# The front of an attention and feed-forward kernel: biases through TensorE, weights one transfer at a time, filling with 512-column products, and a normalisation moved behind a softmax step

## What is computed

```python
def _proj(W, b, x):
    return jnp.einsum('oi,bil->bol', W, x) + b[:, None]
q, k, v = _proj(Wq, bq, ln(x)), _proj(Wk, bk, ctx), _proj(Wv, bv, ctx)     # heads: 8 blocks of 64 columns
scores = jnp.einsum('hbdk,hbek->hbde', qh, kh) / 8
x = x + _proj(Wo, bo, softmax(scores) @ vh)
h = ln(x)
x = x + (silu(h @ deq(gate)) * (h @ deq(up))) @ deq(down)                  # 512 -> 1792 -> 512
deq(w) = (w - zeros of its group) * scales of its group                    # groups of 128 rows
```

## Time and profile before

| | |
|---|---|
| three runs | 451.0, 453.35, 453.71 us; median 453.35 us |
| the profiled execution | 453.45 us, of which the span from first to last instruction is 451.6 us |
| mean granted TensorE clock | 0.981 |
| busy share of the span | PE 93%, ACT 74%, DVE 72%, POOL 60% |
| DMA | 35.52 MB, mean 79 GB/s |
| the front | the first 56 us, up to PE's first L743 |

### The profile page before, as it was taken

One profiled execution on the slowest core, in us unless ns is written; L12 is line 12 of the kernel. 1 busy time (PEld: TensorE's weight loads), 2 busy tenths in 40 slices (PEclk: granted clock), 3 DMA queues, 4 the chain that ended last, 5 costly groups with the idle time before them and its releaser, 6 DMA issues.

```text
span 451.6 us, 10920 instructions
## 1 busy us (share of the span) xinstructions
PE 418.6 (93%) x4318; PEld 328.4 (73%) x4318; DVE 327.0 (72%) x576; ACT 332.9 (74%) x542; POOL 271.4 (60%) x269
## 2 busy tenths in 40 slices
PE   4979898999797799999999899999999999999994
PEld 4857765777584587877777677877778888888873
DVE  2765742999688776878877766877877666666676
ACT  2215699779676788777877858787879999888970
POOL 4145397779858664657555654655656556555561
PEclk8869999999999999999999989999999999999999
DMA  7984343876464100000201000000010000000003
GB/s 196 360 281 137 100 135 129 287 228 228 142 232 137 29 2 25 1 25 1 73 25 48 0 1 25 4 24 3 23 44 6 1 2 0 23 25 23 25 1 93
DMA packets 26918, 35.52 MB, mean 79 GB/s; under 512 B 1963, under 2 KB 18515, under 8 KB 26867
## 3 DMA queue, kind: packets, MB, share of 16 engines
q1 hardware_dynamic: 26354, 34.69, 23.4%
q0 software_dynamic: 192, 0.07, 0.4%
q10 hardware_dynamic: 320, 0.07, 0.1%
HBM read 30.63 MB, written 4.19 MB: 77 GB/s over the span
## 4 chain that ended last, share of the span: by engine, by line
PE 68%; POOL 10%; issue 8%; DVE 5%; ACT 5%; DMA 3%; POOLq 0%; SPq 0%; DVEq 0%; ACTq 0%
PE banks L743 19%; PE banks L745 17%; PE banks L756 9%; PE banks L757 9%; PE banks L641 3%; POOL t_sb L406 3%; PE banks L774 2%; DVE yT L978 2%; POOL hr L419 2%; DMA x_sb<-in_x 2%; PE banks L659 2%; PE banks L681 2%; PE banks L670 2%; PE banks L651 2%; ACT banks L543 1%
## 5 line engine op out<-in xcount | busy, mean ns | idle before, releaser
L543 ACT ACTIVATE banks<-banks,ratio 128x512 f32<-128x512 f32 x336 | 208.3, 665 | 36.9 <-PE banks L745 25.9
L978 DVE SCALAR_TENSOR_TENSOR yT<-banks,sd,yT 128x512 f32<-128x512 f32 x208 | 154.4, 747 | 45.8 <-PE banks L757 45.5
L743 PE MATMUL banks<-xT,wgu 128*128 128x512 f32 x448 | 182.9, 408 | 3.9 <-DVE t_sb L963 2.7
L745 PE MATMUL banks<-xT,wgu 128*128 128x512 f32 x448 | 175.7, 392 | 0.0
L406 POOL TENSOR_TENSOR t_sb<-t_sb,u_sb 128x512 f32<-128x512 f32 x56 | 72.9, 1302 | 92.8 <-DVE t_sb L963 92.5
L743 PEld LDWEIGHTS banks<-xT,wgu 128*128 128x128 f32 x448 | 84.5, 189 | 25.7 <-ACT banks L543 3.3
L756 PE MATMUL banks<-hr,wd 128*128 128x512 f32 x224 | 89.8, 401 | 9.5 <-DVE yT L978 6.1
L745 PEld LDWEIGHTS banks<-xT,wgu 128*128 128x128 f32 x448 | 84.7, 189 | 15.4
L757 PE MATMUL banks<-hr,wd 128*128 128x512 f32 x224 | 87.8, 392 | 0.0
L419 POOL TENSOR_TENSOR hr<-t_sb,hr 128x512 fp32r<-128x512 f32 x56 | 72.2, 1289 | 5.1 <-ACT hr L565 0.7
L756 PEld LDWEIGHTS banks<-hr,wd 128*128 128x128 f32 x224 | 42.2, 188 | 25.7 <-DVE yT L978 13.7
(11 more groups left out here) (88 smaller groups left out, 402.1 us busy)
## 6 DMA issues: line engine op xcount, KB each, us to landing
x_sb<-in_x SPq DMA_DIRECT2D x16, 256.0 KB, 5.4
out<-x_sb SPq DMA_DIRECT2D x16, 256.0 KB, 2.2
wgu_in<-in_L_ffn_gate_w SPq DMA_DIRECT2D x7, 512.0 KB, 6.6
z_in<-in_L_ffn_gate_z SPq DMA_DIRECT2D x7, 512.0 KB, 4.9
wgu_in<-in_L_ffn_up_w SPq DMA_DIRECT2D x7, 512.0 KB, 7.1
z_in<-in_L_ffn_up_z SPq DMA_DIRECT2D x7, 512.0 KB, 5.2
wd_in<-in_L_ffn_down_w SPq DMA_DIRECT2D x7, 512.0 KB, 5.5
z_in<-in_L_ffn_down_z SPq DMA_DIRECT2D x7, 512.0 KB, 4.3
```

The lines of the kernel that those rows point to most:

```text
L543: act.activation(banks[:, bank, :], banks[:, bank, :], ACT.Copy, scale=ratio[:, m, g, it:it + 1]).then_inc(done[n % 2], 1)
L743: pe.matmul(banks[:, bank, :], w, xT[:, c % 2, 0, g, :], start=g == 0, stop=False, skip_group_check=True)
L745: pe.matmul(banks[:, bank, :], w, xT[:, c % 2, 1, g, :], start=False, stop=True, skip_group_check=True).then_inc(full[n % 2], 1)
L978: dve.scalar_tensor_tensor(y, bank, sd[:, it, b:b + 1], y, ALU.mult, ALU.add).then_inc(s_free, 1)
```

## The change

1. **Biases.** POOL's six bias transfers become two. `bv` and `bo` come as one row each from POOL, `bq` and `bk` as one row each from ACT's queue, between the weights `Wq`, `Wk` and `Wv`, `Wo`. PE spreads them: a product of a row of ones with the two rows gives `bq` and `bk` on 128 partitions (L792 of the new file), four products with one column give `bv` and `bo`. DVE copies both results to where they stood before.
2. **Loads.** SP issues context tile 1 and x tile 2 ahead of the scales. For the first four pieces it waits until the integers have landed before it issues the zeros, and until these have landed before it issues the next piece. x tiles 3 to 5 and context tiles 3 to 5 stand in the same list.
3. **Filling.** One `stir` step is now a full float32 product of 512 columns instead of a transpose of 128. The counts go from 16 to 4, from 12 to 3, from 22 to 5, from 7, 6 and 5 to 1.
4. **ACT.** `norm2(j-2)` runs in step j behind the exponential and `norm1`, where it stood at the end of step j-1.
5. **DVE.** `take_w(0)`, which copies the turned `Wq` and `Wk`, runs before `stats(0, 1)`, not behind it.

```diff
@@ sync
-            load_x(0)
-            load_ctx(0)
-            load_x(1)
+            for t in range(2):
+                load_x(t)
+                load_ctx(t)
+            load_x(2)
             sync.dma_start(s_raw[0:NG * NI, 0, :], gate_s.rearrange("g (t p) -> (g t) p", p=P)).then_inc(s_sc, 16)
...
-            load_ctx(1)
-            load_x(2)
-            load_w(0)
-            load_zeros(0)
             load_ctx(2)
             load_x(3)
-            load_w(1)
-            load_zeros(1)
-            load_ctx(3)
-            load_x(PRE)
-            load_ctx(PRE)
-            for k in range(2, NP):
+
+            for k in range(EARLY):
                 load_w(k)
-                if k == 3:
-                    load_x(PRE + 1)
-                    load_ctx(PRE + 1)
+                if 1 <= k < 3:
+                    (load_ctx if k == 1 else load_x)(k + 2)
+                sync.wait_ge(s_w[k], 16)
+                load_zeros(k)
+                if k == 2:
+                    load_ctx(PRE)
+                wait_zeros(sync, k)
+            load_x(PRE + 1)
+            load_ctx(PRE + 1)
+            for k in range(EARLY, NP):
+                load_w(k)
@@ gpsimd
-            for m, v in enumerate((bq, bk)):
-                pool.dma_start(bqk[:, m, :],
-                               v.rearrange("(a o) -> a o", a=1).partition_broadcast(P)).then_inc(s_bias, 16)
-            for h in range(2):
-                for m, v in enumerate((bv, bo)):
-                    pool.dma_start(bvo[h * D:(h + 1) * D, m:m + 1],
-                                   v.rearrange("(o a) -> o a", a=1)).then_inc(s_bvo, 16)
+            pool.memset(ones, 1.0).then_inc(s_id, 1)
+            for m, v in enumerate((bv, bo)):
+                pool.dma_start(b_row[:, 2 + m, :], v.rearrange("(a o) -> a o", a=1)).then_inc(s_bvo, 16)
@@ scalar
             load(s_wsm, wraw[:, 1, :], Wk)
+            for m, v in enumerate((bq, bk)):
+                load(s_bias, b_row[:, m, :], v.rearrange("(a o) -> a o", a=1))
             load(s_wsm2, wraw[:, 2, :], Wv)
...
                 if j + 2 <= PRE:
                     norm1(j + 2)
+                if j >= 2:
+                    norm2(j - 2)
...
                     convert(j - 1)
-                if j >= 1:
+                if j == PRE - 1:
                     norm2(j - 1)
@@ tensor
                 for _ in range(n):
-                    pe.transpose(banks[:, bank, 3 * P:4 * P], ident[:, :], ident[:, :])
+                    pe.matmul(blocks(bank), ident[:, :], ident[:, :].unsqueeze(1).to_broadcast([P, NC, P]),
+                              start=True, stop=True)
             pe.wait_ge(s_id, 2)
-            stir(16)
+            stir(4)
...
-            stir(6)
+            pe.wait_ge(s_id, 4)
+            pe.wait_ge(s_bias, 32)
+            pe.matmul(banks[:, 7, 0:2 * D], ones, b_row[:, 0:2, :], start=True, stop=True).then_inc(s_brow, 1)
+            stir(1)
             pe.wait_ge(s_wT, 1)
             project(0)
-            stir(12)
+            stir(3)
             score(0)
...
+            pe.wait_ge(s_bvo, 32)
+            for m in range(2):
+                for r in HALVES:
+                    mm = pe.matmul(banks[r, 7, 4 * D + m:4 * D + m + 1], b_row[:, 2 + m, :], ones[:, 0:1],
+                                   start=True, stop=True)
             mm.then_inc(s_tr, 1)
...
             turn_x(PRE - 2)
-            stir(22)
+            stir(5)
...
-            stir(7, U_BANK[1])
+            stir(1, U_BANK[1])
@@ vector
+            take_w(0)
             stats(0, 1)
-            take_w(0)
             shift(0, 1)
-            dve.wait_ge(s_bias, 32)
+            dve.wait_ge(s_brow, 1)
+            dve.tensor_copy(bqk[:, :, :].rearrange("p m o -> p (m o)"), banks[:, 7, 0:2 * D]).then_inc(s_bqk, 1)
+            dve.wait_ge(s_bqk, 1)
             take_qk(0, 0)
...
                     take_w(1)
+                    dve.tensor_copy(bvo[:, :], banks[:, 7, 4 * D:4 * D + 2]).then_inc(s_wT, 1)
+                    dve.wait_ge(s_wT, 3)
```

## The result

| | before | changed |
|---|---|---|
| median of the comparison | 452.56 us (4 runs) | 447.20 us (4 runs, 446.94 to 447.67) |
| ratio | | 0.9884, interval 0.9856 to 0.9913 |
| profiled execution, span | 453.45, 451.6 us | 446.94, 445.1 us |
| first feed-forward product | 55.97 us | 50.00 us |

A forecast was written before the change was run, and what follows sets the result against it. PE was taken as nearly the only bound of the front; stage times put its first feed-forward product at 50.1 instead of 55.97 us, carried unchanged to the end: 453.45 - 5.85 = 447.6 us, range 444.5 to 452.5.

The forecast's parts named there:

- Opening: PE's start up to `mix(0)`: projection at 9.0 instead of 10.79, `mix(0)` at 20.0 instead of 21.87, a gain of 1.9 us.
- C: Rival, opening: wide products raise the clock no sooner, it runs at half speed as before; 452.6 us, chance 0.10.
- Price of a filling product: PE's filling: 0.87 us per 512-column product, 1.7 at half clock; five products instead of 22 transposes cost 1.8 us.
- loss of 1.0: At `score(3)`: x tile 4 lands late, q and k are ready at 31.2 where PE could start at 30.2.
- Stall and clock: `mix(0)` to `mix(1)`: the 3.26 us idle and the half clock go, 7.2 us instead of 13.0, `mix(1)` at 27.2.
- Behind weight transfers: The 3.26 us idle in `mix(0)`: PE waits for its own program, held up by weight transfers on the DMA engines.
- B: Rival, `mix(0)`: the stall stays, a matter of PE's list and not of DMA load; 453.2 us, chance 0.12.
- This needs the stall gone: Condition for `mix(1)` 7.7 us earlier: only one 512 KB transfer and a tile in flight from 12 to 40 us.
- Loads one at a time: SP's chain of loads: 4.1 us a step, first integers landing at 10, x tile 4 at 27.4, 1.0 us lost.
- D: Rival, slower: chain of loads too long, PE idles 5 us for x tile 4, clock falls; 454.1 us, chance 0.10.
- E: Rival, main loop takes part back: zeros 4 to 6 come late by 2 to 3 us; 450 us, chance 0.08.
- ACT: Second normalisation moved from in front of tile 2's exponential: exponentials of tiles 2 and 3 come 0.7 us earlier.

The follow-up runs named there:

- after_again: The changed kernel once more, unedited, on another chip: 446.90 us, ratio to before 0.9897.
- x4_early: The changed kernel with x tile 4 issued right behind the first integers and context tile 4 behind the second: 448.89 us, ratio to before 0.9926.
- u_fill: The changed kernel with transposes of 128 columns for filling again, in the old counts: 447.63 us, ratio to before 0.9884.
- x4_lean: As x4_narrow, also without the filling in front of `score(j + 1)` and `values(j)`: 442.69 us, ratio to before 0.9793.
- o_loads: The kernel before with only SP's new list of loads: 449.63 us, ratio to before 0.9946.
- u_bias: The changed kernel with the six bias transfers on POOL's queue again and no bias products on PE: 452.76 us, ratio to before 1.0003.
- x4_bare: As x4_lean, with all filling behind the first 16 transposes dropped: 445.57 us, ratio to before 0.9850.
- u_loads: The changed kernel with SP's old list, the weight transfers issued at once again: 451.78 us, ratio to before 0.9992.
- o_bias: The kernel before with only the biases as rows spread by PE and the two copies on DVE: 449.09 us, ratio to before 0.9941.
- tail3: The changed kernel with three filling products instead of five ahead of the last tile's turning: 445.96 us, ratio to before 0.9858.
- u_norm: The changed kernel with ACT's second normalisation at the end of the step before again: 450.42 us, ratio to before 0.9934.
- x4_narrow: As x4_early, with filling by transposes in the old counts: 443.68 us, ratio to before 0.9800.

## Why the prediction was right, step by step

**The whole.** Forecast 447.6 us, measured 447.2; the first feed-forward product forecast for 50.1, measured at 50.00; faster at 1.2%, to which I gave 0.55. The comparison's own median of before was 452.56, so against it the gain is 5.4 us, and against the profiled execution 453.45 - 446.94 = 6.5 us, where the sum had 5.85.

**Opening.** Four products ended at 7.77 (forecast 7.5), the projection began at 9.62 (9.0), `mix(0)` at 20.13 (20.0). That the engine starts at half speed and rises under the products is what the rows show, and the projection ran at full speed. When it rises is partly luck: the same four products ended at 6.7 us in after_again and at 6.6 in x4_early. What the forecast missed is that narrow filling lets the projection start sooner still, at 7.43 in u_fill. C did not come; it spoke of the half speed "as before", but before the clock had been up at 6.82 and fell again at 8.0.

**Price of a filling product.** Five in a row took 48.65 - 44.36 = 4.29 us, 0.86 each, as forecast (0.87). A single one between other stages takes 1.05, from its start to the next row's. That term was undersized by 0.18 us in each of some 14 places, and nearly all of them are on PE's path. It shows in the first step: `mix(0)` to `mix(1)` took 8.01 us, forecast 7.2, with four fillings at 1.05 and 0.32 us of waiting for DVE, so `mix(1)` came at 28.14 and not at 27.2. It does not show at the end, because the later steps were taken too long: `mix(1)` to `mix(2)` 8.02 (8.65, with a loss of 1.0 that did not come), `mix(2)` to `mix(3)` 5.40 (5.65), the rest 8.44 (8.6). With 0.13 us more in the opening the errors are +0.94 and -1.04 us. That 50.1 met 50.00 so closely is luck.

**Stall and clock.** Right in what it is, and the central point, but only partly right in what sets it. The idle without a semaphore came in the kernel before and in eleven of the twelve experiment kernels after 222, 347 or 348, or 474 records of PE: 126 or 127 records apart, whatever stage stood there; the one after 726 in x4_lean is three such steps behind 348. With its weight load a record is two instructions, so 127 records are some 254. The Trainium skill (Runtime: NRT & Kernel Launch, "Instruction fetch mechanics") has blocks of 16 KiB with 256 instructions and calls the crossing "mostly hidden"; the spacing and the packet's 0.02 MB agree, the hiding does not: 0.2 to 3.3 us were seen here. The instruction queue settles it. In each of these 22 idles (0.17 us and more) PE goes on 1.2 to 1.6 us after the end of a 16 KB packet of that queue (end of the packet and start of PE: 24.39 and 25.70 us in the kernel before, 22.72 and 24.16 in o_loads, 25.29 and 26.85 in after_again), and in the changed kernel's first profile, which has no such idle, the packet had ended 1.7 us before record 347 was due. So PE waits for its program. Two short idles of 0.38 and 0.54 us (after 402 records in u_bias, 796 in x4_bare) have no such packet and are not explained.

"Behind weight transfers" is the part that holds less well. With the weight transfers at once (before, u_loads, o_bias) the packets of the boundaries at 347 or 348 and 474 began 4.0 to 4.2 us after PE had crossed the boundary before, in one case 2.3; with loads one at a time mostly 0.7 to 3.2 us, in one case 4.7. The idles of a front add up to 3.3 to 5.7 us in the first group and to 0 to 2.6 in the second. So crowding goes with longer idles, but they come without it: 2.26 us in o_loads at a DMA share of 0.11, and 1.7 to 2.0 us after 474 records in after_again, tail3, x4_early and u_norm. B, a matter of PE's list, was right to that extent. The step "This needs the stall gone" held for the profiled execution, not for every one.

**Loads one at a time.** x tile 4 was forecast at 27.4; DVE started on it at 27.45. The steps of the chain were 3.7 to 4.1 us. The first integers landed at 11.1 and not at 10, which the shorter steps and a tile that took 4.0 us instead of 4.7 made good. The loss of 1.0 us I had put at `score(3)` did not appear: q and k were ready at 31.2 as forecast, but the longer filling brought PE to `score(3)` at 31.50 only.

**D**, the chain too long, was given 0.10 and did not occur in the profile, but its mechanism did in three others: in u_bias, u_fill and o_loads PE idled 4.0 to 4.3 us for x tile 4, and the clock fell, as the rival had it. In u_norm, tail3 and after_again DVE waited 2.0 to 2.5 us and PE did not idle for it. Against the changed kernel u_bias lost 5.6 us where 6.5 had been worked out. **B** and **E** did not come in the changed kernel; x4_narrow, with a front 5.4 us shorter, did give some back in the main loop, through waits for POOL. **ACT** was right at 0.6 us by the waits (u_norm), with the rest of that run's median open.

## What to carry to other kernels

Price a transfer that is issued behind waits by everything queued behind it: six bias transfers of 0.07 MB cost 5.6 us in the changed kernel, where each piece waits for the last (u_bias), and 0.6%, some 3 us, in the kernel before, which has no such chain (o_bias). Filling on PE is worth its place only up to where the clock holds: transposes in the old counts held it at 1.00 in x4_narrow up to the main loop, and 22 of them cost 2.6 us where five wide products cost 4.3; take the narrow kind, and put the tile that the critical engine needs next at the head of the chain. An idle that no semaphore explains and that stays at the same record count when the code moves points to the engine's own program arriving late; look for the end of a packet of the instruction queue just before the engine goes on.

## What the runs showed of the hardware that I had not expected

The clock fell after shorter idles than I had thought. In x4_bare the idles were 0.2 to 2.6 us long and the clock stood at 0.50 in half of the windows after 20 us; in x4_lean, with idles of 0.4 to 1.9 us and filling at two of four places, it stayed at 1.00 from 11 us on. Nor does one idle decide it: after the same wait in the main loop, 1.86 us in before and 1.88 us in o_loads, the clock read 0.66 from 260 to 265 us in the one and 1.00 from 261.6 to 266.6 us in the other. Executions of one and the same kernel differ by 5 us (after_again, 446.13 to 451.23) and more (u_norm, 446.34 to 453.74), and where two profiles of one kernel exist, the later first feed-forward product comes from the waits at program boundaries (0 against 2.56 us) and the half clock behind them, for about 3 us. x tile 4 took 4.0 us to land in one and 5.2 in the other, and DVE waited 0.55 against 2.53 us for it, without PE idling.
